# One core: row regions, written-out engine orders, late shared parts, routed rows added by VectorE

## The chip, the core and the metric

The kernel runs on one NeuronCore of a Trainium2 chip. The metric is the device time of one execution in microseconds. Three runs of the kernel before took 554.88, 562.25 and 564.08 us; the median is 562.25 us. What differs by less than 2% counts as no change.

## The reference, cut to what matters

8192 tokens (32 batches of 256) of 128 channels, all in float32:

```python
xn = layernorm(x)                       # without gain
# s: a recurrent block on xn
h = ln(xn)*g1+b1; hx = shift(h); xk, xv, xr = mixes of h and hx
k, v = xk @ Wk, xv @ Wv; sr = sigmoid(xr @ Wr)
scan over time: out_t = (e1*aa + e2*v)/(e1*bb + e2); aa, bb decay by exp(w), running max keeps it finite
x2 = xn + (sr*out) @ Wo
h2 = ln(x2)*g2+b2; xk, xr = mixes
s = x2 + sigmoid(xr @ Fr) * (relu(xk @ Fk)**2 @ Fv)       # 512 wide
# g: eight experts, each token goes to the one with the best logit
top = argmax(xn @ gate); score = sigmoid(max(xn @ gate))
g = silu( swiglu_shared(xn) + swiglu_expert[top](xn*score) )   # 256 wide
return x + s*g
```

## The kernel before, in words

The tokens are cut into 16 chunks of 512 (2 batches, 4 tiles of 128). All five engines run their own list of instructions and meet at semaphores.

**Front.** For each chunk SyncE loads x, VectorE takes the statistics (L921, L927), GpSimd makes 1/std with a power (L803 to L809), ScalarE normalises (`first_xn`, L580), TensorE transposes (L341), ScalarE copies the transpose to `XT` (L586), and TensorE makes the router's logits (L351). VectorE chooses each token's expert, and only when all 16 chunks are there it counts, per expert, how many tokens lie before each one, and so which row of the DRAM table `tokens_by_expert` each token gets (`routing_counts`, `routing_starts`, `routing_rows`, L960 to L988). The table has 71 tiles of 128 rows; it is first filled with padding rows by one DMA of 4686 KB.

**Steps.** Then come 18 steps, the same function `step(i)` on each engine. Step i advances the recurrent block of three chunks at once: z1 transpose, key, value, receptance of chunk i+1 (L366 to L387), the scan of chunk i on VectorE (L1010 to L1054), attention output, second norm, `ffn_key` of chunk i-1 (L396 to L419), `ffn_value` of chunk i-2 (L427). Each step has eight places where other work is filled in by `plan()`: in steps 0 to 5 the shared expert's 32 half parts (L449, L455 gate and up, L437 down, L1106), while GpSimd sends the rows to the table with one indirect DMA for each of 64 tiles (L849), 12 in a step; in steps 6 to 14 the 71 expert slots; in the last three steps the final sums.

**An expert slot** loads a tile of rows and its expert's weights (SyncE), scales the rows by the score (ScalarE, L683), transposes them (L478), multiplies by gate and up (L471), takes silu (L692) and the product (VectorE, L1114), multiplies by down (L485), copies out (L700), and scatters the rows to `routed_out` (GpSimd, L857).

**End.** For each chunk TensorE adds the routed rows and the shared output in PSUM by two products with the identity (L498, L499), ScalarE takes silu (L707), VectorE multiplies by s (L1121). Chunks 0 to 11 are added to a copy of x in DRAM by GpSimd's accumulating DMA (L868); the other four are added on VectorE and stored by SyncE. The block of the squares: `relu` of four quarters on ScalarE (L658), squares of quarters 0 and 2 on ScalarE (L666), of 1 and 3 on VectorE (L1090). The present token's weight comes from a tanh (L616), and needs the two 1024-wide products L1046 and L1049.

## Time and profile before

| | |
|---|---|
| three runs | 554.88, 562.25, 564.08 us |
| profiled execution | span 552.1 us from first to last instruction; its own device time isn't listed apart from these runs |
| PE | 477.2 us busy, 86% |
| VectorE | 401.3 us, 73% |
| ScalarE | 353.4 us, 64% |
| GpSimd | 279.0 us, 51% |
| granted TensorE clock, mean | 0.977 |
| DMA | 64.97 MB, 118 GB/s over the span |

A float32 matmul leaves two records in this trace (L471 has 568 for 284 products), a transpose one. Records overlap, since matmuls are pipelined: the time that one takes out of TensorE is the distance from its start to the next start, not its length.

### The profile page before, as it was taken

What the parts mean: (1) busy time and instruction counts of PE and PEld (TensorE: products, weight loads), DVE (VectorE), ACT (ScalarE), POOL (GpSimd) and SP (SyncE); (2) the same over time, 40 slices, a digit from 0 to 9 for tenths busy, and PEclk for the clock granted to TensorE, in tenths of its full rate; (3) what the DMA queues carried; (4) which work ended last, traced back from release to release, by engine and by line L of the source; (5) the groups of instructions that cost most, each with busy time, mean ns of one, the idle gap of its engine ahead of it and who ended that gap; (6) DMA issues with size and microseconds to landing.
All of it is one profiled execution on the core that took longest, in us unless ns stands there. A gap on an engine that the chain in (4) does not pass through costs nothing. (4 is left out here: it accounts for less than half of the span.)

```text
span 552.1 us, 9051 instructions
## 1 busy us (share of the span) xinstructions
PE 477.2 (86%) x2687; PEld 356.4 (65%) x2687; DVE 401.3 (73%) x808; ACT 353.4 (64%) x707; POOL 279.0 (51%) x329
## 2 busy tenths in 40 slices
PE   1989877879998789979898989898989898869796
PEld 1989444547575556569686868686868777644454
DVE  3553697858795877858696969797878788875345
ACT  4777424656663748576878686969696968554542
POOL 7565003565756375735273737363646464634440
PEclk9999898998999999989999999999999999999799
DMA  6339508210101010126363737373737372438395
GB/s 210 102 89 248 121 0 300 108 42 13 44 20 44 1 49 12 49 55 174 114 202 111 208 106 207 101 216 94 225 100 211 102 207 92 118 115 134 69 184 109
DMA packets 62592, 64.97 MB, mean 118 GB/s; under 512 B 5776, under 2 KB 50705, under 8 KB 62496
## 3 DMA queue, kind: packets, MB, share of 16 engines
q1 hardware_dynamic: 50736, 51.16, 32.5%
q0 software_dynamic: 10656, 11.68, 9.3%
q10 hardware_dynamic: 1152, 1.56, 0.9%
q8 instruction: 22, 0.36, 0.3%
q14 instruction: 26, 0.21, 0.1%
HBM read 46.86 MB, written 21.12 MB: 123 GB/s over the span
## 5 line engine op out<-in xcount | busy, mean ns | idle before, releaser
L857 POOL DMA_INDIRECT routed_out<-xh,xs x71 | 91.1, 1283 | 52.5 <-ACT xh L700 34.9
L849 POOL DMA_INDIRECT tokens_by_expert<-xn,pos x64 | 70.3, 1098 | 35.1 <-issue 18.5
L471 PE MATMUL bank_ring<-xh,ew 128*128 128x128 f32 x568 | 76.8, 279 | 0.0
L471 PEld LDWEIGHTS bank_ring<-xh,ew 128*128 128x128 f32 x568 | 70.8, 194 | 4.5 <-issue 3.8
L1090 DVE TENSOR_TENSOR kk<-rk 128x512 f32<-128x512 f32 x32 | 24.2, 755 | 61.2 <-ACT rk L658 55.6
L427 PE MATMUL bank_out<-fvw,kk 128*128 128x128 f32 x512 | 67.5, 278 | 0.0
L427 PEld LDWEIGHTS bank_out<-fvw,kk 128*128 128x128 f32 x512 | 63.4, 195 | 3.9 <-issue 3.9
L692 ACT ACTIVATE px<-bank_ring 128x256 f32<-128x256 f32 x71 | 27.1, 381 | 36.7 <-PE bank_ring L471 31.3
L831 POOL TENSOR_SCALAR x_sm<-x_mv 128x4 f32<-128x4 f32 x16 | 4.0, 247 | 81.4 <-DVE x_mv L1071 81.4
L485 PE MATMUL bank_ring<-ew,hx 128*128 128x128 f32 x284 | 43.5, 276 | 0.0
L387 PE MATMUL bank_fa<-xr,att 128*128 128x512 f32 x32 | 18.3, 656 | 24.6 <-ACT rk L658 23.8
L1114 DVE TENSOR_TENSOR hx<-px,bank_ring 128x256 f32<-128x256 f32 x71 | 29.1, 409 | 13.9 <-ACT px L692 13.9
L437 PEld LDWEIGHTS bank_ring<-sdn,hs 128*128 128x128 f32 x256 | 31.4, 194 | 11.9 <-issue 6.5
L455 PE MATMUL bank_ring<-xt,sup 128*128 128x512 f32 x64 | 34.8, 626 | 3.8 <-DVE hs L1106 3.8
L485 PEld LDWEIGHTS bank_ring<-ew,hx 128*128 128x128 f32 x284 | 37.3, 191 | 0.8 <-issue 0.7
L845 POOL TENSOR_TENSOR rw<-den_num,lq 128x512 f32<-128x512 f32 x16 | 20.2, 1262 | 33.8 <-issue 27.1
L449 PE MATMUL bank_ring<-xt,sup 128*128 128x512 f32 x64 | 34.3, 619 | 2.3 <-ACT tg L676 2.3
L419 PE MATMUL bank_fb<-xk,fkw 128*128 128x512 f32 x64 | 33.5, 604 | 1.8 <-issue 1.5
L437 PE MATMUL bank_ring<-sdn,hs 128*128 128x128 f32 x256 | 31.7, 278 | 3.4 <-DVE hs L1106 3.4
L700 ACT ACTIVATE xh<-bank_ring 128x256 f32<-128x256 f32 (+1 forms) x75 | 27.8, 371 | 9.6 <-PE bank_ring L485 6.8
L580 ACT ACTIVATE xn<-xi,nb,rs 128x128 f32<-128x128 f32 x64 | 26.3, 483 | 11.5 <-POOL nb L809 11.5
L419 PE MATMUL bank_fa<-xk,fkw 128*128 128x512 f32 x64 | 32.8, 594 | 0.0
(143 smaller groups left out, 1145.4 us busy)
## 6 DMA issues: line engine op xcount, KB each, us to landing
ew<-ex_w SPq DMA_DIRECT2D x71, 384.0 KB
xi<-x SPq DMA_DIRECT2D x20, 256.0 KB, 2.8
tokens_by_expert<-pad_row SPq DMA_DIRECT2D x1, 4686.0 KB, 20.4
xs<-tokens_by_expert SPq DMA_DIRECT2D x71, 66.0 KB
ew<-routed_out SPq DMA_DIRECT2D x16, 256.0 KB, 3.1
out<-xn POOLq DMA_DIRECT2D x12, 256.0 KB, 6.0
routed_out<-xh,xs POOLq DMA_INDIRECT x71, 2.9
tokens_by_expert<-xn,pos POOLq DMA_INDIRECT x64
```

The lines of the kernel that those rows point to most:

```text
L419: nc.tensor.matmul((FA, FB)[q % 2][:, :], part(FKW, q, P), XK2[:, :], start=True, stop=True)\
L427: last = nc.tensor.matmul(part(BO, j, CH), KK[:, q * CHUNK + j * P:q * CHUNK + (j + 1) * P], part(FVW, q, CH), start=(q + j == 0), stop=(q ...
L437: last = nc.tensor.matmul(part(b, j, CH), h[:, q * CHUNK + j * P:q * CHUNK + (j + 1) * P], part(SDN, q, CH), start=(q == 0), stop=(q == EQ ...
L449: nc.tensor.matmul(ring(5 * m + 3 * q)[:, :], part(SUP, q, P), part(XT, m, CHUNK), start=True, stop=True)\
L455: nc.tensor.matmul(ring(5 * m + 3 * q + 1)[:, :], part(SUP, EQ + q, P), part(XT, m, CHUNK), start=True, stop=True).then_inc(s_su, 1)
L471: last = nc.tensor.matmul(part(GU[n % 2], q, P), part(w, q, P), xt[:, 0:P], start=True, stop=True)
L485: last = nc.tensor.matmul(BX[:, P:P + CH], part(h, q, P), part(w, 2 * EQ + q, CH), start=(q == 0), stop=(q == EQ - 1))
L692: nc.scalar.activation(PX[n % 2][:, :], GU[n % 2][:, 0:EF], ACT.Silu).then_inc(s_px, 1)
L700: nc.scalar.activation(XH[n % NXH][:, a:b], BX[:, a:b], ACT.Copy).then_inc(s_xh, 1)
L849: nc.gpsimd.indirect_dma_start(xs_dram, bass.IndirectOffsetOnAxis(ap=POS[:, t:t + 1], axis=0), XN[:, t * XROW:(t + 1) * XROW], None).then_ ...
L857: nc.gpsimd.indirect_dma_start(routed_dram, bass.IndirectOffsetOnAxis(ap=XS[(n - 2) % NXS][:, CH:CH + 1].bitcast(i32), axis=0), XH[n % NXH ...
L1114: nc.vector.tensor_tensor(HX[n % NHX][:, :], PX[n % 2][:, :], GU[n % 2][:, EF:2 * EF], ALU.mult)\
```

## The change

It does many things at once.

- **Row regions.** Every expert has a region of 8320 rows of its own in the DRAM table, plus seven spare tiles. A row's place no longer depends on the counts of all experts, so rows are chosen after every four chunks (`expert_choice`, `expert_rows`), and their scatters can be sent from then on. Padding is 7 spare tiles and 8 tails of 66 KB in place of the 4686 KB fill. SyncE reads each tile's first row from a table.
- **Written-out orders.** `plan()`, `fill` and `step` go; each engine's calls are written out one by one. The first norm, the shared parts and the recurrent block's first chunks are interleaved. Between the first two and the last two of the 71 slots stand 15 slots to 2 chunks.
- **Late shared parts.** Shared parts of chunks 11 to 15 come after the last expert slot; their down products accumulate onto the routed rows in the same bank.
- **Routed rows on VectorE.** For chunks 0 to 10 VectorE adds routed rows to the shared output; for 11 to 15 one identity product stays.
- **Arithmetic moved.** Score scaling goes from ScalarE to GpSimd, all four squares to ScalarE, three small operations of the first norm from GpSimd to VectorE; exp with a clamp takes the place of tanh, and one 1024-wide VectorE operation goes. Receptance has two buffers and may run further ahead.
- 13 chunks, not 12, are added in DRAM; x is copied to the output before the routing is known.

```diff
+GROUPS = CHUNKS // GROUP
 
 XTILES = TILES + EXPERTS - 1
+REGION = TOKENS + P
+SPARE = XTILES - TILES
+XROWS = EXPERTS * REGION + SPARE * P
 XROW = CH + 4
...
+EARLY = 11
+ADDED = 13
+SUMS = list(range(CHUNKS))
+ON_VECTOR = (0, 1, 2, 3, 4, 5, 6, 7, 8, 9, 10)
...
+            sp.wait_ge(s_pad, 2)
+            sp.dma_start(xs_dram[EXPERTS * REGION:XROWS, :].rearrange("(n p) c -> p n c", p=P),
+                         PAD[:, :].unsqueeze(1).to_broadcast([P, SPARE, XROW])).then_inc(s_fill, 16)
...
-                if c == CHUNKS - 1:
-                    sp.wait_ge(s_pad, 2)
-                    sp.dma_start(xs_dram.rearrange("(n p) c -> p n c", p=P),
-                                 PAD[:, :].unsqueeze(1).to_broadcast([P, XTILES, XROW])).then_inc(s_fill, 16)
...
+                r = nc.sync.value_load(ROW[0:1, n:n + 1], min_val=0, max_val=XROWS - P)
+                sp.dma_start(XS[n % NXS][:, :], xs_dram[bass.ds(r, P), :]).then_inc(s_xs[n % NXS], 16)
...
-            sp.wait_ge(s_rt, RT_DONE)
+            sp.dma_start(out[0:ADDED * CHUNK // 2, :], x[0:ADDED * CHUNK // 2, :]).then_inc(s_pre, 16)
+            sp.dma_start(out[ADDED * CHUNK // 2:ADDED * CHUNK, :], x[ADDED * CHUNK // 2:ADDED * CHUNK, :]).then_inc(s_pre, 16)
+            sp.wait_ge(s_map, 1)
+            for e in range(EXPERTS):
+                r = nc.sync.value_load(PADS[0:1, e:e + 1], min_val=0, max_val=EXPERTS * REGION - P)
+                sp.dma_start(xs_dram[bass.ds(r, P), :], PAD[:, :]).then_inc(s_tail, 16)
...
             def receptance(c):
                 pe.wait_ge(s_mix, 3 * c + 3)
-                if c > 1:
-                    pe.wait_ge(s_rk, 4 * c - 5)
+                if c > 2:
+                    pe.wait_ge(s_rk, 4 * (c - 3) + 3)
...
+            def late_part(m, q):
+                if (m, q) == (EARLY, 0):
+                    pe.wait_ge(s_hx, XTILES)
+                    pe.wait_ge(s_xh, XTILES + 4)
+                else:
+                    pe.wait_ge(s_tg, 2 * m + q)
+                nc.tensor.matmul(RING[0][:, :], part(SUP, q, P), part(XT, m, CHUNK), start=True, stop=True)\
+                  .then_inc(s_sg, 1)
+                pe.wait_ge(s_hs, 2 * m + q)
+                nc.tensor.matmul(RING[1][:, :], part(SUP, EQ + q, P), part(XT, m, CHUNK),
+                                 start=True, stop=True).then_inc(s_su, 1)
...
-                    pe.wait_ge(s_hs, 2 * CHUNKS)
-                    pe.wait_ge(s_sh, CHUNKS)
+                    pe.wait_ge(s_hs, 2 * EARLY)
+                    pe.wait_ge(s_sh, EARLY)
...
-                    nc.tensor.matmul(b[:, :], ident, RR[c % 4], start=True, stop=False)
-                    nc.tensor.matmul(b[:, :], ident, part(XT, c, CHUNK), start=False, stop=True).then_inc(s_fy, 1)
...
+            def final_sum(m):
+                p = SUMS.index(m)
+                pe.wait_ge(s_fr_in[p % 4], 16 * (p // 4 + 1))
+                if any(n not in ON_VECTOR for n in SUMS[:p]):
+                    pe.wait_ge(s_fw, p)
+                else:
+                    pe.wait_ge(s_hx, XTILES)
+                    pe.wait_ge(s_xh, XTILES + 4)
+                b = RING[2]
+                nc.tensor.matmul(b[:, :], ident, RR[p % 4], start=True, stop=False)
+                if m < EARLY:
+                    nc.tensor.matmul(b[:, :], ident, part(XT, m, CHUNK), start=False, stop=True).then_inc(s_fy, 1)
+                    return
+                pe.wait_ge(s_hs, 2 * m + 2)
+                h = HS[m % 2]
+                for j in range(TPC):
+                    for q in range(EQ):
+                        last = nc.tensor.matmul(part(b, j, CH), h[:, q * CHUNK + j * P:q * CHUNK + (j + 1) * P],
+                                                part(SDN, q, CH), start=False, stop=(j + q == TPC + EQ - 2))
+                last.then_inc(s_fy, 1)
 
...
+            z1_transpose(5)
+            ffn_value(2, 0)
+            value(4)
+            ffn_value(2, 1)
+            expert_slot(3)
+            attention_out(3)
+            ffn_value(2, 2)
+            expert_slot(4)
+            ffn_value(2, 3)
+            expert_slot(5)
+            key(5)
+            receptance(5)
...
-            def tanh_d(c):
-                act.wait_ge(s_d, c + 1)
+                act.wait_ge(s_dc, c + 1)
                 if c > 0:
                     act.wait_ge(s_num, c)
-                nc.scalar.activation(TT, DD[:, :], ACT.Tanh, scale=0.5).then_inc(s_tt, 1)
+                nc.scalar.activation(QQ, DD[:, :], ACT.Exp).then_inc(s_q, 1)
 
...
-            def scale_rows(n):
-                act.wait_ge(s_xs[n % NXS], 16 * (n // NXS + 1))
-                xs = XS[n % NXS]
-                nc.scalar.activation(xs[:, 0:CH], xs[:, 0:CH], ACT.Identity, scale=xs[:, CH + 1:CH + 2])\
-                  .then_inc(s_xsc, 1)
...
+                if t % GT == 0:
+                    pool.wait_ge(s_pos, t // GT + 1)
+                    pool.wait_ge(s_sc, t // GT + 1)
...
+            def scale_rows(n):
+                pool.wait_ge(s_xs[n % NXS], 16 * (n // NXS + 1))
+                xs = XS[n % NXS]
+                nc.gpsimd.tensor_scalar(xs[:, 0:CH], xs[:, 0:CH], xs[:, CH + 1:CH + 2], None, ALU.mult).then_inc(s_xsc, 1)
...
+            def keep_logits(c):
+                dve.wait_ge(s_lg, c + 1)
+                nc.vector.tensor_copy(part(LG, c, TPC * E), BO[:, 0:TPC * E]).then_inc(s_lc, 1)
...
+            def expert_rows(g):
+                a, b = g * GT, (g + 1) * GT
+                first = CST[:, K_REG:K_REG + E] if g == 0 else part(BEGIN, g, E)
+                dve.wait_ge(s_th, g + 1)
+                nc.vector.tensor_scalar(rows_of_xn[:, a:b, CH + 1], part(SC, g, GT), 0.5, 0.5, ALU.mult, ALU.add)\
+                  .then_inc(s_sc, 1)
+                dve.wait_ge(s_rm, g + 1)
+                link(nc.vector.tensor_tensor(place, BO[:, 0:E], first, ALU.add))
+                link(nc.vector.tensor_tensor(part(BEGIN, g + 1, E), BO[:, E:2 * E], first, ALU.add))
+                link(nc.vector.tensor_tensor(cum, cum, place.unsqueeze(2).to_broadcast([P, E, GT]), ALU.add))
+                link(nc.vector.tensor_tensor(CUM, CUM, OH, ALU.mult))
+                link(nc.vector.tensor_reduce(POSF[:, a:b], CUM.rearrange("p (e j) -> p j e", e=E), AX.X, ALU.add))
+                nc.vector.tensor_copy(POS[:, a:b], POSF[:, a:b]).then_inc(s_pos, 1)
...
-                nc.vector.scalar_tensor_tensor(batches(DD[:, :]), before(PP), vec(V_FIRST), batches(BK[:, :]),
-                                               ALU.subtract, ALU.subtract).then_inc(s_d, 1)
-
-            def wkv_b(c):
+                    dve.wait_ge(s_q, c)
+                nc.vector.tensor_tensor(batches(DD[:, :]), batches(BK[:, :]), before(PP), ALU.subtract).then_inc(s_d, 1)
...
+            def present_value(c):
+                dve.wait_ge(s_q, c + 1)
+                dve.wait_ge(s_v, c + 1)
+                nc.vector.tensor_tensor(N2, QQ, BV[:, :], ALU.mult).then_inc(s_n2, 1)
...
-                tt = batches(TT).unsqueeze(1).to_broadcast([P, 2, BPC, SEQ])
-                nc.vector.scalar_tensor_tensor(dn, tt, 1.0, ba, ALU.add, ALU.mult).then_inc(s_w1b, 1)
-                dve.wait_ge(s_w1b, c + 1)
+                qv = QV[:, :].rearrange("p (k b t) -> p k b t", k=2, b=BPC)
                 dve.wait_ge(s_n2, c + 1)
-                nc.vector.tensor_tensor(DN[:, :], DN[:, :], TV[:, :], ALU.subtract).then_inc(s_num, 1)
+                nc.vector.tensor_tensor(dn, ba, qv, ALU.add).then_inc(s_num, 1)
...
-            def ffn_square(c, q):
-                dve.wait_ge(s_rk, 4 * c + q + 1)
-                if q == 1 and c > 0:
-                    dve.wait_ge(s_kv, c)
-                rk = part(RK, 1, CHUNK)
-                nc.vector.tensor_tensor(part(KK, q, CHUNK), rk, rk, ALU.mult).then_inc(s_kd, 1)
...
+            def final_sum(m):
+                p = SUMS.index(m)
+                dve.wait_ge(s_fr_in[p % 4], 16 * (p // 4 + 1))
+                dve.wait_ge(s_sh, m + 1)
+                nc.vector.tensor_tensor(part(XT, m, CHUNK), part(XT, m, CHUNK), RR[p % 4], ALU.add).then_inc(s_fd, 1)
```

## Rows read from the trace of the kernel before

**Rows 1.** Windows: PE, PEld, DVE, ACT, POOL busy (count), clock, DMA share, GB/s.

```profile
0.00:62.00 62.00, 47.19 (x206) 42.96 (x206) 30.21 (x159) 38.08 (x91) 33.98 (x87) 1.00 0.65 171
62.00:243.00 181.00, 155.19 (x723) 96.83 (x723) 140.14 (x240) 103.70 (x169) 95.42 (x99) 0.97 0.17 56
243.00:478.00 235.00, 214.33 (x1530) 181.62 (x1529) 191.33 (x341) 176.59 (x390) 122.75 (x120) 0.99 0.51 152
478.00:552.00 74.00, 60.52 (x232) 34.96 (x230) 39.58 (x70) 34.98 (x59) 26.84 (x24) 0.92 0.62 114
```

**Rows 2.** The chain that ended last: start us, us, what.

```profile
499.70 0.86 PE bank_ring L499 x2
502.27 0.89 PE bank_fb L408 x8
```

**Rows 3.** Timeline of TensorE, front and one expert slot: start us, us, instruction.

```profile
44.20 1.09 PE L341 MATMUL bank_out<-consts,xn 128*128 128x128 f32 x4
45.09 1.71 PE L351 MATMUL bank_fb<-gw,xt 128*128 128x8 f32 x8
46.65 1.09 PE L341 MATMUL bank_v<-consts,xn 128*128 128x128 f32 x4
...
250.33 1.06 PE L471 MATMUL bank_ring<-xh,ew 128*128 128x128 f32 x8
251.22 0.27 PE L478 MATMUL bank_ring<-consts,xs 128*128 128x128 f32 x1
251.33 0.61 PE L485 MATMUL bank_ring<-ew,hx 128*128 128x128 f32 x4
251.78 1.06 PE L427 MATMUL bank_out<-fvw,kk 128*128 128x128 f32 x8
```

**Rows 4.** Timeline of TensorE, one whole step of the expert stretch.

```profile
270.84 1.05 PE L396 MATMUL bank_fb<-att,rw 128*128 128x128 f32 x8
...
296.94 1.10 PE L387 MATMUL bank_fa<-xr,att 128*128 128x512 f32 x2 [1.81 <-ACT rk L658]
297.87 1.05 PE L396 MATMUL bank_fb<-att,rw 128*128 128x128 f32 x8
```

**Rows 5.** Groups by line and form: busy us, mean ns, idle before.

```profile
L683 ACT ACTIVATE xs<-xs 128x128 f32<-128x128 f32 x71 | 28.0, 398 | 0.0
...
L1090 DVE TENSOR_TENSOR kk<-rk 128x512 f32<-128x512 f32 x32 | 24.2, 755 | 61.2 <-ACT rk L658 55.6 <-issue 5.6
...
L1049 DVE TENSOR_TENSOR den_num<-den_num,tanh_d_and_value 128x1024 f32<-128x1024 f32 x16 | 19.6, 1225 | 0.6
```

**Rows 6.** The same view, GpSimd's scatters.

```profile
L857 POOL DMA_INDIRECT routed_out<-xh,xs x71 | 91.1, 1283 | 52.5 <-ACT xh L700 34.9 <-issue 17.6
...
L849 POOL DMA_INDIRECT tokens_by_expert<-xn,pos x64 | 70.3, 1098 | 35.1 <-issue 18.5 <-DVE kk L984 16.6
```

**Rows 7.** Timeline of GpSimd: the first scatter, then one step's small work.

```profile
83.74 1.27 POOL L849 DMA_INDIRECT tokens_by_expert<-xn,pos  x1 [16.56 <-DVE kk L984]
...
275.16 0.23 POOL L831 TENSOR_SCALAR x_sm<-x_mv 128x4 f32<-128x4 f32 x1 [5.20 <-DVE x_mv L1071]
...
277.01 1.04 POOL L823 TENSOR_TENSOR d<-h 128x512 f32<-128x512 f32 x1
278.21 1.81 POOL L857 DMA_INDIRECT routed_out<-xh,xs  x1 [0.17 <-issue]
...
295.73 1.26 POOL L845 TENSOR_TENSOR rw<-den_num,lq 128x512 f32<-128x512 f32 x1 [1.80 <-issue]
```

**Rows 8.** Timeline of VectorE: a scan that starts beside GpSimd's L823.

```profile
277.20 1.93 DVE L1034 TENSOR_TENSOR_SCAN bb_aa<-e,ev 128x514 f32<-128x514 f32 x1
```

**Rows 9.** By source: L823, then L1034: ns min/median/max, first and last start.

```profile
L823 POOL TENSOR_TENSOR d<-h x16: 1033/1040/2003, 51.1 to 466.2; 128x512 f32<-128x512 f32 x16
...
L1034 DVE TENSOR_TENSOR_SCAN bb_aa<-e,ev x16: 1202/1751/1956, 71.8 to 490.9; 128x514 f32<-128x514 f32 x16
```

**Rows 10.** Timeline of TensorE, its last matmul.

```profile
546.21 1.02 PE L499 MATMUL bank_ring<-xt,consts 128*128 128x512 f32 x2
```

More of the change, by code:

```diff
@@ L27 @@
 NEG = -1e38
+DMAX = 40.0
 NXS, NEW, NXH, NHX, AHEAD = 12, 5, 8, 3, 4
@@ new lines, in _ @@
+            pe.wait_ge(s_w, 16 * 3)
+            first_transpose(0)
+            z1_transpose(0)
+            logits(0)
+            first_transpose(1)
+            pe.wait_ge(s_wa, 16 * 5)
+            shared_part(0, 0)
+            logits(1)
+            first_transpose(2)
+            pe.wait_ge(s_wa, 16 * 5)
+            key(0)
+            logits(2)
+            first_transpose(3)
+            receptance(0)
+            value(0)
+            logits(3)
+            first_transpose(4)
+            z1_transpose(1)
@@ new lines, in _ @@
+            receptance(2)
+            shared_part(5, 0)
+            routing_prefix(2)
+            z1_transpose(3)
+            first_transpose(15)
+            logits(14)
+            value(2)
+            shared_part(5, 1)
+            pe.wait_ge(s_half, 1)
+            attention_out(0)
+            logits(15)
+            shared_part(6, 0)
+            routing_prefix(3)
+            shared_part(6, 1)
+            z2_transpose(0)
+            key(3)
+            shared_part(7, 0)
+            ffn_key(0, 0)
@@ new lines, in _ @@
+            ffn_key(4, 3)
+            ffn_value(4, 1)
+            expert_slot(18)
+            attention_out(5)
+            ffn_value(4, 2)
+            expert_slot(19)
+            ffn_value(4, 3)
+            expert_slot(20)
+            receptance(7)
+            key(7)
+            expert_slot(21)
+            z2_transpose(5)
+            value(7)
+            expert_slot(22)
+            z1_transpose(8)
+            ffn_receptance(5)
+            ffn_key(5, 0)
+            expert_slot(23)
@@ new lines, in _ @@
+            key(9)
+            expert_slot(36)
+            z2_transpose(7)
+            value(9)
+            expert_slot(37)
+            z1_transpose(10)
+            ffn_receptance(7)
+            ffn_key(7, 0)
+            expert_slot(38)
+            ffn_key(7, 1)
+            ffn_key(7, 2)
+            expert_slot(39)
+            ffn_key(7, 3)
+            ffn_value(7, 0)
+            expert_slot(40)
+            attention_out(8)
+            expert_slot(41)
+            receptance(10)
@@ new lines, in _ @@
+            ffn_key(8, 3)
+            ffn_value(8, 1)
+            expert_slot(48)
+            attention_out(9)
+            ffn_value(8, 2)
+            expert_slot(49)
+            ffn_value(8, 3)
+            expert_slot(50)
+            receptance(11)
+            key(11)
+            expert_slot(51)
+            z2_transpose(9)
+            value(11)
+            expert_slot(52)
+            z1_transpose(12)
+            ffn_receptance(9)
+            ffn_key(9, 0)
+            expert_slot(53)
```

2142 lines of the change are left out of this document (1692 added, 450 removed).

## The prediction, made before the result was known

> **What bounds the kernel now.** I read the windows first, cut where the work changes: the first norm (0 to 62), the stretch with shared parts and scatters (to 243), the 71 expert slots (to 478), the end (to 552) [rows 1]. TensorE is the busiest engine in all four, but its busy time overstates its load, so I price it by distances between starts. A 512-wide product takes 0.86 us, four 128-wide ones 0.89 [rows 2]. In the front, four transposes take 0.89 (44.20 to 45.09) and a chunk's logits 1.56 (45.09 to 46.65); an expert slot takes 1.45 (250.33 to 251.78), 0.11 of it for one transpose [rows 3].
>
> From these a chunk costs, beside its front: z1 and z2 transposes 0.44 each, key, value and receptance 2.58, attention output 0.89, FFN receptance 0.89, four keys 3.44, sixteen value products 3.56: together 12.2 us. Its shared part costs 5.2 (four at 0.86, eight at 0.22), its two identity products 1.7. The whole program: 16 x (2.45 + 12.2 + 5.2 + 1.7) = 345, and 71 x 1.45 = 103: 448 us of 552. So 104 us are idle or at the lower clock.
>
> Where they lie: one step in the expert stretch runs from 270.84 to 297.87, 27.0 us [rows 4], with 12.2 + 8 x 1.45 = 23.8 us of matmuls. 3.2 us are lost, 1.8 of them in one wait of the receptance for ScalarE's last relu, which stands behind a table load, Ln and Exp. Over the 8.7 steps from 243 to 478 that is some 28 us. The front to 243 holds 16 x 2.45 + 16 x 5.2 + six chunks x 12.2 = 195 us: 48 are lost, most of them before 97, where the first scatter waited 16.6 us for VectorE's routing and started only at 83.7 [rows 7]. The rest is lost at the end, whose clock is 0.92 [rows 1].
>
> **The change part by part.**
>
> *The identity products.* 32 become 5: 27 x 0.86 = 23 us less for TensorE, all in the end, where TensorE is what bounds. VectorE gets 11 sums of the form of L1090 (0.755 us, 0.6 by distance): 7 us, on an engine busy for 39.6 of the last 74 us [rows 1, 5]. TensorE's total becomes 448 - 23 = 425 us.
>
> *Arithmetic.* VectorE loses two squares (1.5 us) and one 1024-wide operation (1.2) per chunk [rows 5]. The clamp is new: no row has it; between half and all of L1090's 0.755, I take 0.45, as it is one pass over the same 512 columns. Net -2.2 us per chunk. ScalarE loses 0.40 per slot for the scaling [rows 5] and gains two squares, near 0.6 each by L1090's size: 7.5 x 0.4 - 1.2 = 1.8 us less per chunk. Exp for tanh I cost at nothing (ScalarE has 58 of 235 us free). Both are off the path; they shorten what stands ahead of the waits in the step.
>
> *GpSimd's scaling.* No row has 128 x 128 there. Nearest are L831 (4 columns, 0.23) and L823 (512 columns, two inputs, 1.04) [rows 7]: between 0.23 and 1.04; on the line between them 0.43, which I take. A scatter out takes (91.1 + 17.6)/71 = 1.53 with its issue time [rows 6]. Per chunk: 7.5 x (1.53 + 0.43) = 14.7, and the norm's small operations with d1, 275.16 to 278.21, 3.1, and rw 1.3 [rows 7]: 19.1 us, below the 23 of TensorE. With 1.04 per row it would be 23.7.
>
> *The front.* Rows of chunks 0 to 3 can be sent once logits 0 to 3 and one small routing round are done. VectorE has 30.2 us up to 62 now, for 16 norms, four choices and chunk 0 up to its differences [rows 1]; its new list has 11 norms with five more small operations each, one choice, chunk 0 to its scans and three half parts ahead of the first rows, which I put at 36; the x loads and the hops between engines make it about 45 (ends: 40, and 84 as now). From there GpSimd's one queue sets the pace: 64 scatters at (70.3 + 18.5)/64 = 1.39 make 89 [rows 6]; among them stand five powers (5.5), three rw (3.8), and three rounds of the small operations and d1 (9.3): 108 us, to 153. Then landing, SyncE's loads of rows, and the first scaling, which the run shows only in pieces: 7 us. The slots start at **160**, against 243. Does the rest fit under it? TensorE has 16 x 2.45 + 11 x 5.2 + 32 for parts of chunks 0 to 4 = 128; VectorE 170.3 now to 243 [rows 1], less ten late products (7), less 2.5 chunks x 18.7 ((191.3 - 29)/8.7) = 47, less 8 for lighter arithmetic, plus some 10 for more small routing and norm operations: 119. Both fit. The smaller fill (4686 KB to 7 tiles and 8 tails) and the earlier copy of x leave the queue before loads that matter; eight tails and 71 row lookups on SyncE are covered, since a slot leaves it over 3 us and needs two issues.
>
> *The slots.* Between first and last stand 15 slots to two chunks: 12.2 + 7.5 x 1.45 = 23.1 us of matmuls per chunk. The relus no longer stand behind Ln and Exp and the receptance waits for an older relu, so its 1.8 us goes; what comes next is ScalarE's silu and copy, which TensorE needs within the slot. I keep 1.4 us of loss: 24.5 (ends: 23.1 and 27.0). From slot 0 to slot 72 TensorE's list has 71 x 1.45 + 119.5 of chunk work = 222 us; at 23.1/24.5 it takes **241**, to 401.
>
> *The end.* After slot 72 stand 44 us of chunk work, ten half parts at 1.72 (17) and five final sums at 0.86 + 1.78 (13): 74 us. VectorE has 65 in the same stretch: 11 sums, 19 final operations and ten half parts at 0.6 are 24, and 2.5 chunks at 18.7 - 2.2 are 41. The last chunks' recurrences have nothing left to hide behind but these. I take 85, the share of idle time of the present end with less clock lost (ends: 79 and 95). From TensorE's last matmul (547.2) to the end of the span are 4.9 us now [rows 10]; I take 5.
>
> **Sum:** 160 + 241 + 85 + 5 = 491 us of span, against 552.1. The fastest run is 2.8 above that span and the median 10.1; I add 6: **497 us**.
>
> **A rule against it.** An L823 of 1.04 us at 277.01 and a scan beside it from 277.20, which took 1.93 where its least is 1.20; L823 itself goes from 1.03 to 2.00 [rows 7, 8, 9]. So the two engines hold each other up, for about the length of one instruction, and the change gives GpSimd 71 more instructions on SBUF. The Trainium skill, SBUF — State Buffer, section SBUF: two separate sides, has it that a VectorE operation with two SBUF inputs, or in a two-port mode, and a GpSimd operation that reads SBUF exclude each other for the whole instruction; by that rule the trace agrees, and a clamp in a two-port mode would also hold back GpSimd's descriptors.
>
> **The rivals.**
> - *The ports bite.* Ten GpSimd operations per chunk (7.5 scalings and three others) each wait 0.7 us, the delay of that scan: 19.1 + 7 = 26.1 us per chunk, 241 x 26.1/24.5 = 257: 513. Against: 108 of 235 us are free on GpSimd, and not every one meets a long operation. 0.05.
> - *Late front.* Four engines in fixed order hold VectorE's first routing round to 80, as now [rows 7]: slots start at 195, 532. For: VectorE was idle half of the first 62 us [rows 1]. Against: 36 us of work. 0.12.
> - *The step stays at 27.0* per chunk because another wait replaces the receptance's: 241 x 27.0/24.5 = 266: 522. 0.13.
> - *All goes well:* start 150, 231 for the slots, 79 at the end: 150 + 231 + 79 + 5 + 6 = 471. 0.08.
> - *Nothing gained.* Late front, step of 27.0, and an end of 95: 195 + 266 + 95 + 5 + 6 = 567, within 2%. 0.04.
> - *Slower.* GpSimd becomes the bound of the slots: every operation of it, scatters included, is doubled, as the longest L823 was: 38 us per chunk, 241 x 38/24.5 = 374: 630. It decides from 32 us per chunk on (1.7 times), where 573 is passed. Against: the mean scatter was 1.28 and 1.10, with VectorE at 81% [rows 1, 6]. 0.03.
> - The forecast: 0.55.
>
> **Range and chances.** About 2% can be told from no change. The range takes in the forecast, both neighbours at 513 and 522, the good case at 471 and the late front at 532: 470 to 533. Faster: all cases but "nothing gained" and "slower", 0.93; same 0.04; slower 0.03.
>
> **What would show it.** In the changed profile: the first scatter near 45 us and the last near 153; the first L1114-like product near 160; starts of attention outputs 24.5 us apart on average between slots 7 and 67; last expert product near 401; GpSimd's scaling near 0.43 us; TensorE's last matmul near 486. The prediction is wrong if the slots start after 195, if the chunks are 27 us apart, or if GpSimd is over 90% busy between 160 and 401.

## The result, and the profile after

The changed kernel took 527.49 us (median of four runs, 519.34 to 530.05), the kernel before 558.57 us on the same chip (four runs, 552.61 to 564.08). The ratio is 0.947, 95% interval 0.933 to 0.960: faster. The ratio goes by the runs within 1.5% of the fastest of their kernel (519.34 and 526.38 of the changed one), and the profiled run, 528.60, isn't one of them. The forecast was 497 from a median of 562.25, a gain of 65 us; 31 were measured. The profiled execution has a span of 526.8 us against 491 forecast; 35.8 us have to be found.

The page of the changed kernel (busy time, then tenths in 40 slices):

```profile
PE 448.2 (85%) x2645; PEld 336.9 (64%) x2645; DVE 398.6 (76%) x907; ACT 339.1 (64%) x661; POOL 329.9 (63%) x347
...
PE   0968969788199989899999989998999887497995
...
DVE  4599978488348289968996896799599989884452
...
PEclk9979968859779999999999999999999998798998
```

GpSimd has 51 us more than before, as scaling came to it. TensorE has two thin places, slice 11 (132 to 145) and slice 35 (448 to 461), and the clock is low around both and around 100 to 120. By windows, cut where the work changes as [rows 1] are (columns as there):

```profile
0.00:62.00 62.00, 41.98 (x199) 28.68 (x200) 48.37 (x230) 35.63 (x79) 36.97 (x38) 0.94 0.34 104
62.00:185.00 123.00, 98.45 (x456) 66.12 (x455) 78.53 (x192) 61.94 (x113) 82.45 (x84) 0.82 0.27 87
185.00:418.00 233.00, 221.26 (x1558) 184.16 (x1557) 199.74 (x357) 178.56 (x362) 174.49 (x189) 1.00 0.52 153
418.00:526.00 108.00, 86.47 (x437) 57.90 (x436) 72.00 (x131) 62.94 (x110) 35.95 (x38) 0.92 0.44 79
```

The start moved from 243 to 185 and the stretch of slots kept its length (233 against 235), although 71 scalings moved and the mixture of work in it is other. The end grew from 74 to 108, as it now holds the late shared parts that stood in the front. The same by source (ns least, median, most; first and last start): expert products, scatters, scalings, first powers, scans of the weighted values, sums on VectorE, clamps, and the product that makes z1.

```profile
L480 PE MATMUL bank_ring<-xh,ew x568: 272/275/275, 185.3 to 418.5; 128*128 128x128 f32 x190
...
L1607 POOL DMA_INDIRECT tokens_by_expert<-xn,pos x64: 957/962/1932, 50.1 to 174.4; - x64
...
L1614 POOL TENSOR_SCALAR xs<-xs x71: 598/713/1882, 180.6 to 406.6; 128x128 f32<-128x128 f32 x71
...
L1572 POOL TENSOR_TENSOR rs<-ve,minus_half x16: 1627/1642/2483, 8.3 to 74.8; 128x8 f32<-128x8 f32 x16
...
L2081 DVE TENSOR_TENSOR_SCAN bb_aa<-e,ev x16: 1214/1216/1229, 45.4 to 470.6; 128x514 f32<-128x514 f32 x16
...
L2172 DVE TENSOR_TENSOR xt<-xt,ew x11: 656/684/1761, 432.5 to 465.7; 128x512 f32<-128x512 f32 x11
...
L2066 DVE TENSOR_SCALAR dd<-dd,vectors x16: 485/486/829, 29.9 to 465.3; 128x512 f32<-128x512 f32 x16
...
L2036 DVE TENSOR_TENSOR z<-xn,r x16: 668/1255/2136, 13.2 to 410.4; 128x512 f32<-128x512 f32 x16
```

The scalings by group (busy us, mean ns, idle before):

```profile
L1614 POOL TENSOR_SCALAR xs<-xs 128x128 f32<-128x128 f32 x71 | 58.3, 825 | 6.3 <-DMA xs<-tokens_by_expert 4.6
```

So against the forecast's terms: start 185.3 for 160 (+25), slots 233 for 241 (-8), end from 418.5 to 526.8, 108 for 90 (+18).

What the thin place at 132 to 145 is, the timelines of TensorE, ScalarE and VectorE say (start us, us, instruction; in brackets the idle time before it and who ended it):

```profile
133.22 1.12 PE L414 MATMUL bank_fb<-xk,fkw 128*128 128x512 f32 x2 [1.73 <-issue]
134.19 1.02 PE L414 MATMUL bank_fa<-xk,fkw 128*128 128x512 f32 x2
145.25 2.08 PE L414 MATMUL bank_fb<-xk,fkw 128*128 128x512 f32 x2 [10.05 <-ACT rk L999]
...
144.60 0.60 ACT L999 ACTIVATE rk<-bank_fb 128x512 f32<-128x512 f32 x1 [11.44 <-remote]
...
150.85 0.69 DVE L2146 TENSOR_TENSOR hs<-tg,bank_ring 128x512 f32<-128x512 f32 x1 [14.49 <-PE bank_ring L464]
```

TensorE issued the key product at 133.2, and ScalarE, whose relu needs nothing else that was still open, started only at 144.6. "remote" stands where the profile names no instruction that ended at that time. I call this a late count: TensorE's count of a finished product (its semaphore) reached the others late. That the product itself ended late can't be excluded, as the ends of matmuls are modelled. TensorE then waited for ScalarE's relu and VectorE for the shared part behind: one such stop, and three engines stand for 10 to 14 us. All such rows of the list of waits, 60 to 200:

```profile
ACT rk L999 <- remote: 12.2, 2, 11.4
ACT xt L930 <- remote: 6.3, 1, 6.3
DVE rt L1999 <- remote: 4.8, 1, 4.8
DVE ew L1972 <- remote: 4.1, 2, 3.0
ACT tf L993 <- remote: 2.4, 1, 2.4
```

The thin place in the end, TensorE and VectorE:

```profile
445.59 1.02 PE L444 MATMUL bank_ring<-xt,sup 128*128 128x512 f32 x2
454.53 2.07 PE L447 MATMUL bank_ring<-xt,sup 128*128 128x512 f32 x2 [7.91 <-DVE hs L2157]
...
450.88 0.66 DVE L2172 TENSOR_TENSOR xt<-xt,ew 128x512 f32<-128x512 f32 x1
451.46 1.22 DVE L2097 TENSOR_TENSOR den_num<-bb_aa,q_and_q_value 128x1024 f32<-128x1024 f32 x1
452.60 0.68 DVE L2178 TENSOR_TENSOR xn<-xt,xn 128x512 f32<-128x512 f32 x1
453.20 0.68 DVE L2102 SCALAR_TENSOR_TENSOR den_num<-tr,den_num 128x512 f32<-128x512 f32 x1
453.80 0.68 DVE L2157 TENSOR_TENSOR hs<-tg,bank_ring 128x512 f32<-128x512 f32 x1
```

TensorE waits 7.9 us for the late product of chunk 11, which stands on VectorE behind final sums (L2172), final products (L2178) and a recurrence. This was the first suspect for the end, and the very thing that the title of the change puts there.

### The profile page after: what moved, and what is told of

It reads as the page before. It is cut to its first block, busy times and chain, and to the rows that moved or that the text cites. A ratio compares the mean times of both kernels' runs of the same rounds, so it can differ in the third digit from the quotient of the medians.

```text
span 526.8 us, 9495 instructions
## 1 busy us (share of the span) xinstructions
PE 448.2 (85%) x2645; PEld 336.9 (64%) x2645; DVE 398.6 (76%) x907; ACT 339.1 (64%) x661; POOL 329.9 (63%) x347
## 4 chain that ended last, share of the span: by engine, by line
PE 38%; ACT 9%; DVE 4%; issue 4%; POOL 1%; ACTq 0%; POOLq 0%; DVEq 0%
PE bank_ring L480 8%; PE bank_out L424 6%; PE bank_ring L494 4%; PE bank_fb L414 4%; PE bank_fa L414 3%; PE bank_fb L391 2%; PE bank_k L367 2%; PE bank_fb L403 1%; PE bank_fb L397 1%; PE bank_ring L487 1%; PE bank_fa L382 1%; PE bank_ring L447 1%; PE bank_ring L444 1%; PE bank_ring L515 1%; ACT e L953 1%
## 5 line engine op out<-in xcount | busy, mean ns | idle before, releaser
L1619 POOL DMA_INDIRECT routed_out<-xh,xs x71 | 81.4, 1147 | 43.9 <-issue 24.6
L1607 POOL DMA_INDIRECT tokens_by_expert<-xn,pos x64 | 67.9, 1061 | 21.1 <-issue 21.1
L480 PE MATMUL bank_ring<-xh,ew 128*128 128x128 f32 x568 | 74.9, 275 | 0.0
L1614 POOL TENSOR_SCALAR xs<-xs 128x128 f32<-128x128 f32 x71 | 58.3, 825 | 6.3 <-DMA xs<-tokens_by_expert 4.6
L1005 ACT ACTIVATE kk<-rk 128x512 f32<-128x512 f32 x64 | 40.3, 650 | 0.7
L1572 POOL TENSOR_TENSOR rs<-ve,minus_half 128x8 f32<-128x8 f32 x16 | 28.5, 1786 | 15.7 <-DVE ve L1936 15.6
L978 ACT ACTIVATE z<-x,x_sm 128x128 f32<-128x128 f32 x64 | 26.4, 482 | 17.0 <-POOL x_sm L1592 16.9
L464 PE MATMUL bank_ring<-xt,sup 128*128 128x512 f32 x44 | 28.9, 745 | 3.3 <-DVE hs L2146 3.3
L2146 DVE TENSOR_TENSOR hs<-tg,bank_ring 128x512 f32<-128x512 f32 x22 | 15.0, 680 | 20.4 <-PE bank_ring L464 16.5
L1631 POOL DMA_DIRECT2D out<-xn x13 | 17.2, 1831 | 19.1 <-DVE xn L2178 18.0
```

Source lines behind the costliest of these rows:

```text
L464: nc.tensor.matmul(ring(5 * m + 3 * q + 1)[:, :], part(SUP, EQ + q, P), part(XT, m, CHUNK), start=True, stop=True).then_inc(s_su, 1)
L480: last = nc.tensor.matmul(part(GU[n % 2], q, P), part(w, q, P), xt[:, 0:P], start=True, stop=True)
L1005: nc.scalar.activation(part(KK, q, CHUNK), part(RK, q % 2, CHUNK), ACT.Square).then_inc(s_kk, 1)
L1572: nc.gpsimd.tensor_tensor(RS[:, a:b], VE[:, a:b], NH[:, 0:2 * TPC], ALU.pow).then_inc(s_rs, 1)
L1607: nc.gpsimd.indirect_dma_start(xs_dram, bass.IndirectOffsetOnAxis(ap=POS[:, t:t + 1], axis=0), XN[:, t * XROW:(t + 1) * XROW], None).then_ ...
L1614: nc.gpsimd.tensor_scalar(xs[:, 0:CH], xs[:, 0:CH], xs[:, CH + 1:CH + 2], None, ALU.mult).then_inc(s_xsc, 1)
```

## The experiments

Seventeen runs (e1 and e13 are the changed kernel itself), in groups that share one chip and their runs of the kernel before. Ratios are to that kernel, with their 95% intervals.

**First group: is it there again, and what do the sums cost.** The kernel before took 547.46.

> The changed kernel once more, as a control. In its profile TensorE stood still from 134.6 to 144.6 (fourth key of chunk 0 waits for a relu whose product had been issued at 134.2) and had a late count at 96 to 106. If the program sets these two stops (its instructions, its order), they come again within 3 us of the same places and the slots start at 185 +- 3. If they are accidents of one execution (a page of DRAM, a refresh), they are gone or elsewhere, the slots start near 170, and that profile is some 10 to 15 us shorter. Ratio to the kernel before 0.947 +- 0.013.

No edit. 509.46 us, ratio 0.929 (0.925 to 0.934), span 508.0. Its expert products, and its one wait of TensorE over 4 us in the front:

```profile
L480 PE MATMUL bank_ring<-xh,ew x568: 272/275/275, 169.3 to 401.2; 128*128 128x128 f32 x190
...
142.65 1.11 PE L397 MATMUL bank_fb<-consts,z 128*128 128x128 f32 x4 [5.20 <-ACT z L978]
```

Not one row of "remote" stands between 60 and 200. The start is 16 us earlier, slots (231.9) and end (106.8) are as they were. So 16 of the 35.8 us belong to the execution, not to the program. Against its own kernel before (547.46) the changed one gains 38 us here, still far from 65.

> The named part of the change alone is undone: the sums of chunks 0 to 10 are two identity products each on TensorE (11 x 2 x 0.86 = 19 us more for it), and VectorE has eleven operations of 0.6 less. My prediction: TensorE bounds the end, so the end is 19 us longer: 546, ratio to the kernel before 0.98. Rival A: VectorE bounds 432 to 454 (the 7.9 us wait of TensorE for the late product), so the products fill TensorE's idle time there: only 19 - 12 = 7 us longer, 534. Rival B: the sums on VectorE cost more than they spare: 527 or less.

```diff
-ON_VECTOR = (0, 1, 2, 3, 4, 5, 6, 7, 8, 9, 10)
+ON_VECTOR = ()
...
@@ tensor @@
 ffn_receptance(12)
+final_sum(0)
 ffn_key(12, 0)
+final_sum(1)
...
```

521.46 us, ratio 0.952 (0.948 to 0.957): 12.0 us more than e1, for 19 us of products. Slots 167.7 to 399.6; all of it lies in the end. Between my sum (19) and rival A (7): TensorE bounds the end for most of the time, not all of it. Its waits after the last slot add up to 11.8 us here and to 17.3 in e1, so 5.5 us of the products went into waits. The named part of the change is worth 12 us.

> 24 products of 8 columns (four instructions each, 96 in all, into a bank that nothing reads) stand ahead of TensorE's list, where it waits for the first x anyway. Theory, code loading: the stops at 96 and 134 stand where TensorE's next block of 256 instructions is fetched, so that both move 96 instructions earlier in its list (the second one from the third key of chunk 0 to before the first shared part of chunk 6, near 118), or vanish. Rival, the queue of transfers: the stop at 134 stands beside the eight tail writes of SyncE (133 to 148) and stays with them. Rival, the order: it stays at the fourth key of chunk 0. Time: 527 +- 8 by each, as one stop takes the place of the other; 517 if they vanish.

```diff
 pe.wait_ge(s_w, 16 * 3)
+for _ in range(24):
+    nc.tensor.matmul(RING[2][:, 0:EXPERTS], ident, GW[:, :], start=True, stop=True)
```

513.60 us (0.936), start 173.3, 4 us behind e1. No late count at all, here as in its control: inconclusive.

> SyncE writes the eight tails of 66 KB after the first five blocks of expert weights (384 KB each) instead of before them. Theory, the queue of transfers: with 8 x 128 short rows no longer at 133 the stop of TensorE at 134.6 to 144.6 goes, slots start near 175, 517 us. Rival, code loading or order: the stop stays within 3 us, 527 +- 8, and only the weights land earlier (before 149).

```diff
-for e in range(EXPERTS): ...  # eight tails
 for n in range(NEW):
     load_weights(n)
+for e in range(EXPERTS): ...
```

510.74 us (0.932), start 169.6: the place of the tails is worth nothing. On the late counts it is as inconclusive as e3.

**Second group: the end.** Before 546.55.

> VectorE's late product (11, 0) stands ahead of the first final sum instead of behind ten sums, nine final products and den_num. In the control (508.0) TensorE waits for it in the end and runs at the lower clock after. Theory, the named wait is the cause: TensorE goes on about 8 us earlier, 501. Rival, VectorE's load is the cause (it is busy without a gap for 22 us there, with z2 of chunk 13 and the mixes of chunk 15 behind the same work): the wait only moves to the next step, 508 +- 2. From the times of both: what TensorE needs next, z2 of chunk 13, came 1.7 us after the late product, so I expect the rival, ratio to the kernel before 0.929 +- 0.004.

```diff
@@ vector @@
 channel_mixes(12)
+late_part(11, 0)
 final_sum(0)
...
-late_part(11, 0)
 time_mixes(15)
```

510.85 us (0.934; 0.932 to 0.937). This group has no control of its own; e8, whose end is untouched, took 509.37. As the rival had it: the named wait is gone and the next one stands in its place, as long.

```profile
436.55 1.11 PE L397 MATMUL bank_fb<-consts,z 128*128 128x128 f32 x4 [8.84 <-ACT z L978]
```

> Part left out: VectorE's eleven final sums add one column instead of 512, so chunks 0 to 10 of the output lack nearly all of the routed part; waits and order are unchanged. If VectorE bounds 413 to 437, this is 11 x 0.45 = 5 us shorter, of which 8 or 9 sums stand in the stretch: 504. If the sums lie beside other work, as my prediction had it (7 us on VectorE, hidden), no change: 508.

```diff
-nc.vector.tensor_tensor(part(XT, m, CHUNK), part(XT, m, CHUNK), RR[p % 4], ALU.add)
+nc.vector.tensor_tensor(XT[:, m*CHUNK:m*CHUNK+1], XT[:, m*CHUNK:m*CHUNK+1], RR[p % 4][:, 0:1], ALU.add)
```

510.72 us (0.936; 0.933 to 0.938): nothing gained. Even without the width of the sums TensorE waits 7.71 us at 435.8. On VectorE:

```profile
425.72 0.69 DVE L2179 TENSOR_TENSOR xn<-xt,xn 128x512 f32<-128x512 f32 x1 [0.93 <-ACT xt L1041]
...
427.52 0.68 DVE L2135 SCALAR_TENSOR_TENSOR xi<-tf,bank_out 128x512 f32<-128x512 f32 x1
...
430.58 0.67 DVE L2112 TENSOR_TENSOR x<-bank_fb,xn 128x512 f32<-128x512 f32 x1
```

The freed time became idle time (0.93 here): in 413 to 435 VectorE is busy for 16.85 us, against 21.75 in e1, and 3.5 us of the rest it waits for ScalarE's silu of the final sums (L1041). And x2 of chunk 13 (L2112) still came at 430.6, 5 us after its product, behind s of chunk 12 (L2135) and a scan. My theory that the sums themselves make the end long fell, and with it the simpler one that VectorE's load does: with 4.9 us less of it TensorE still waits. What holds x2 back here is its place in VectorE's list, which e9 changes.

> The same sums and final products by the same engines, but those of chunks 5 to 10 come after the last recurrence, where VectorE idles (20 of the last 67 us in the control), with chunks 11 and 12 between them; the late product (11, 0) first and d1 of chunk 15 ahead of the norm of chunk 13. If VectorE's load in 413 to 437 is the cause of the long end, 12 operations of 0.6 leave it: 7 us and what the lower clock took there (1 to 3): 499. If the end is bound by the chain of recurrences through ScalarE's table loads, nothing: 508. If the stores or ScalarE's order become late: slower, up to 513.

```diff
-SUMS = list(range(CHUNKS))
+SUMS = [0, 1, 2, 3, 4, 11, 5, 6, 12, 7, 8, 9, 10, 13, 14, 15]
@@ vector @@
 make_tn(15)
+final_sum(5)
+final_sum(6)
+final_sum(7)
+final_sum(8)
...
```

The late product (11, 0) and d1 of chunk 15 move forward as well.

514.12 us (0.940; 0.937 to 0.943), 3 to 5 us slower than its neighbours. The reason named last fits: moved that far, the sums hold up the final sums of TensorE, which run in one order with them and now wait 3.3 us for ScalarE's L1041. TensorE's waits after the last slot add up to 20.5 us, against 17.1 in e5, and its clock there is 0.90.

```profile
436.14 1.11 PE L397 MATMUL bank_fb<-consts,z 128*128 128x128 f32 x4 [8.52 <-ACT z L978]
...
474.56 2.05 PE L507 MATMUL bank_ring<-ew,consts 128*128 128x512 f32 x2 [3.30 <-ACT xt L1041]
```

> Front, GpSimd's order: rw of chunk 2 and the norm's small operations of chunk 1 stand four scatters earlier. In the control their inputs are there at 132.2 and they start at 138.4, and TensorE waits 5.2 us for z2. If TensorE sets the start of the slots, it comes 5 us earlier (164); if the scatters and loads behind them set it (last scatter 157.4, first scaled rows 165), 0 to 2.5 us: start 167 to 169. I expect the latter: 507, not to be told from no change; TensorE's wait for z2 of chunk 1 below 1 us.

```diff
@@ gpsimd @@
 scatter_rows(47)
+make_rw(2)
+rstd_of_x2(1)
...
 scatter_rows(51)
-make_rw(2)
-rstd_of_x2(1)
```

509.37 us (0.933), start 168.3 for 169.3: no change that can be told, as expected. TensorE's wait for z2 of chunk 1 is gone (no wait over 0.2 us between 130 and 150) and the start did not follow: scatters and loads set it.

**Third group: two edits of the order, and the scaling.** Before 553.74. Late counts in all four: "remote" rows add up to 29 to 35 us in 60 to 200, the slots start at 179.8 to 182.3. So these are compared by stage: last slot to the end of the span.

> End. Leaving the sums out (e6), moving them later (e7) and the late product forward (e5) shortened nothing: in all of them z2 of chunk 13 came at 436 to 438, as x2 of chunk 13 stands on VectorE behind s of chunk 12 and a scan, 3 to 7 us after its product (425), and GpSimd's norm and d1 of chunk 15 behind that. Here x2 of chunk 13 stands ahead of them, the late product (11, 0) ahead of the sums, d1 of chunk 15 and the norm of chunk 13 ahead of the stores of chunks 5 to 7, and z2 of chunk 13 ahead of ScalarE's eighth final part. Theory, the chain of chunk 13 sets TensorE's wait of 8.3 us: it shrinks to about 3, 503 (ratio to the kernel before 0.920). Rival, the chain of chunk 15 (its recurrence, weighted values to tn) sets the end: 508 to 510 as it is now (0.930).

```diff
@@ vector @@
 channel_mixes(12)
+late_part(11, 0)
 final_sum(0)
...
 final_sum(7)
+make_x2(13)
...
@@ gpsimd @@
 final_store(4)
+make_d1(15)
+rstd_of_x2(13)
...
```

ScalarE's and VectorE's final parts of chunk 8 move back behind z2 of chunk 13 and the mixes.

523.51 us (0.947; 0.943 to 0.951); end 413.3 to 520.6, 107.3 against 106.8 in e1. The wait for z2 is 5.2, where it was 8.8 in e5, another joined it, and nothing was gained. VectorE had no gap in the stretch: 21.75 of 22 us busy (the window below, columns as above). TensorE's timeline, then the window:

```profile
446.36 1.12 PE L397 MATMUL bank_fb<-consts,z 128*128 128x128 f32 x4 [5.20 <-ACT z L978]
448.86 2.07 PE L367 MATMUL bank_k<-xk,att 128*128 128x512 f32 x2 [1.39 <-DVE xk L2044]
```

```profile
425.00:447.00 22.00, 12.79 (x67) 8.47 (x68) 21.75 (x38) 16.81 (x30) 12.55 (x13) 0.94 0.97 195
```

> End. ScalarE's fourth relu of chunk 13 stands ahead of the table load, Ln, Exp and second table load for chunk 15 (4 us) instead of behind them. In the control TensorE waits 3.1 us for that relu before the attention output of chunk 14, then works without a wait to the last product but for 0.7 us. Theory, every wait of TensorE there is paid in full: 505 (0.924). Rival, the late product (13, 0), which ScalarE's four microseconds now stand ahead of, makes TensorE wait instead: 508 (0.930).

```diff
@@ scalar @@
-preload("natural_log_exp_and_others"); inverse_of_den(15); preload("silu_and_others")
 ffn_relu(13, 3)
 late_part(12, 1)
 ffn_square(13, 3)
 final_part(11)
+preload("natural_log_exp_and_others"); inverse_of_den(15); preload("silu_and_others")
```

521.47 us (0.943; 0.938 to 0.948), end 415.6 to 520.6: 105.0. TensorE's wait of 3.1 us is gone, waits of 0.9 and 0.3 came; 2 us gained of 3. (Nine profiles of kernels whose end was not changed have ends of 106.7 to 110.1 us.)

> The reordering of e8 (rw of chunk 2 and norm of chunk 1 four scatters earlier), of e9 and of e10 together. If the waits of the end are paid by themselves, 508 - 5 - 3 - 1 = 499 (0.913); if one of them takes the place of the other, 503 (0.920).

Edit: e8, e9 and e10 together. 519.16 us (0.936; 0.929 to 0.942), end 103.0: 3.8 us less than in e1, more than e9 and e10 gave one by one.

> One part undone: the 71 scalings of rows are done by ScalarE (0.40 each in the kernel before) instead of GpSimd (0.83 on average in the changed one), each right behind the copy of its slot. My prediction: ScalarE has room and so has GpSimd, so that the place of the scaling is off the path: slots from 169 to 401 as before, 508 (0.930). Rival, ScalarE's silu and copy, which TensorE needs within the slot, come 0.4 us later in each: 1 us per chunk more, 518 (0.947). Rival, the ports: with 71 fewer operations of GpSimd on SBUF VectorE's longest operations (2.0 us against 0.7 to 1.2) get rarer, and the slots take 3 us less: 505.

```diff
@@ scalar @@
+def scale_rows(n):
+    act.wait_ge(s_xs[n % NXS], 16 * (n // NXS + 1))
+    nc.scalar.activation(xs[:, 0:CH], xs[:, 0:CH], ACT.Identity, scale=xs[:, CH + 1:CH + 2])...
@@ gpsimd @@
-scale_rows(n)   # all 71
```

526.03 us (0.952; 0.948 to 0.956). Slots 180.3 to 416.9, 236.6 us, against 233.5 and 233.8 in e9 and e10: the scaling on GpSimd is worth 3 us, a third of the 10 that the first rival had. The rival of the ports has the wrong sign on balance. VectorE is busy for 202.0 us in the slots without the scalings and for 198.2 (e9) and 199.1 (e10) with them, so no cost of theirs shows on VectorE either.

**Fourth group.** Before 546.88.

> The changed kernel again, as the control of this group. The chips so far are of two kinds: on two of them the kernel before takes 547 us and the changed one, where it ran, 509 (0.929), with no late count of TensorE; on two others the kernel before takes 554 to 559 and changed kernels 519 to 527, with late counts in the front (4 to 10 us before 150) and slots that start 12 to 16 us later. If the late counts belong to the chip, this is either 509 and start 169, or 522 and start 180; the ratio 0.929 or 0.943.

510.75 us, 0.933 (0.931 to 0.935), start 168.5, no "remote" row.

> As all three reorderings together (e11), and the sums and final products of chunks 6 to 8 stand behind the mixes of chunk 15 and of chunk 13. In e9 VectorE was without a gap from 425 to 452 and TensorE's key of chunk 15 waited for the mixes (1.4) behind z2 (5.2). If VectorE's load bounds that stretch, 6 operations of 0.6 less ahead of the mixes give 3 to 4 us beyond e11; if the chain of chunk 15 behind them bounds, nothing. I expect 2 us less than e11.

```diff
@@ vector, on top of e11 @@
...
 channel_mixes(13)
+final_sum(6)
+final_sum(7)
+final_sum(8)
 final_sum(9)
 running_max(15)
+final_part(6)
+final_part(7)
 differences(15)
+final_part(8)
 final_part(9)
...
```

The same calls go from their old places, and ScalarE's final parts 6 and 7 move back behind z2 of chunk 13.

504.14 us, ratio 0.923 (0.919 to 0.926): the fastest of all, 6.6 us below its control. Key of chunk 15 follows z2 without a wait:

```profile
433.39 1.11 PE L397 MATMUL bank_fb<-consts,z 128*128 128x128 f32 x4 [5.26 <-ACT z L978]
434.30 1.91 PE L367 MATMUL bank_k<-xk,att 128*128 128x512 f32 x2
```

> The 24 small products ahead of TensorE's list (96 instructions) once more. On a chip with late counts they stood, in three kernels with the same TensorE list, before 91, 107 and 149. Code loading: the places in the list move 96 instructions earlier or the counts are in time; anything else: the same products are late again. On a chip without them it tells nothing new: 4 us above the control.

512.15 us (0.936), again without late counts: inconclusive a second time.

> The three reorderings together, beside their control now. In its first run the end from the last slot took 103.0 us against 106.8, 107.3 and 106.7 of the control, e9 and e12. 4 us below the control by that: ratio to it 0.992.

506.26 us, ratio 0.925 (0.923 to 0.928), 4.5 below its control: 0.991, as expected. From e16 to e14 are 2.1 us more, but the runs of both overlap (505.19 to 507.79, 503.39 to 506.84) and the ends in their profiles are 102.8 and 102.3: that moving the three sums helps further isn't shown.

**Fifth group.** Before 554.32.

> Part left out: GpSimd's first power takes the 4 columns of 1/sqrt(var + eps) and not the other 4 (the factor for z1 is 1 instead), so z1 of the attention part is scaled wrongly; waits and order are unchanged. In the control the power of 8 columns takes 1.64 (16 of them, 26 us), where my forecast had 1.1. Theory, this size is what makes the front late: 16 x 0.6 less on the engine that sets the first and the last scatter, of which 11 stand ahead of the first (where it waits for VectorE now and then) and 5 among the scatters: first scatter at 48 to 49 instead of 51.2, last 3 us plus that earlier, near 152, slots from 164 instead of 169. Rival, TensorE's list of shared parts sets the start: slots from 168 or 169, 509.

```diff
-nc.gpsimd.tensor_tensor(RS[:, a:b], VE[:, a:b], NH[:, 0:2 * TPC], ALU.pow)
+nc.gpsimd.tensor_tensor(RS[:, a:a + TPC], VE[:, a:a + TPC], NH[:, 0:TPC], ALU.pow)
```

518.90 us (0.937; 0.927 to 0.948, the widest interval of all). This chip is the one of the fourth group, where the kernel before took 546.9; now it takes 554.3 and counts come late. So the late counts do not belong to a chip, as I had thought in e13. The powers fell to 1.01 us, but the first scatter stayed at 50.9 and GpSimd waited for VectorE instead (25.0 us against 16.4):

```profile
L1573 POOL TENSOR_TENSOR rs<-ve,minus_half x16: 1006/1012/1852, 8.4 to 75.9; 128x4 f32<-128x4 f32 x16
...
  DVE ve L1937: 25.0, 11
```

The three longest late counts of this run, of eight rows in its list of waits:

```profile
ACT xt L930 <- remote: 5.9, 1, 5.9
DVE ew L1973 <- remote: 4.8, 2, 3.0
DVE hs L2147 <- remote: 4.8, 1, 4.8
```

The last scatter was at 167.9 and the start at 179.1, against 168.3 and 179.8 in e9. By this comparison (both with late counts, on two chips) the size of the power is not what makes the front late.

## Why the prediction was off, point by point

**The shape held.** The start moved forward, the slots kept their pace, TensorE stayed the engine that bounds, GpSimd took the scaling. Slots: 241 forecast, 232 to 234 measured in every run of this order. 241 was a slip: 222 at 23.1/24.5 is 236. The pace itself was right: from 183.4 to 379.6 the attention outputs of e1 start 24.5 us apart, as forecast. The other 4 us are work that I had placed in the slots and that stands behind them: at my prices the products recorded between first and last slot come to 217 us, not 222. "The ports bite" and "slower" did not come: GpSimd is busy for 174.5 of 233 us in the slots. Scaling has a median of 0.71 and a mean of 0.83, where I took 0.43, and was still hidden, as e12 shows. The scan of [rows 8, 9], with a median of 1.75 before, has 1.22 in the changed kernel, but the stall did not go: the product that makes z1 (L2036), never over 0.69 before (L995), now has a median of 1.26 and takes up to 2.14. Another instruction meets GpSimd's now, and the slots kept their pace all the same. Clamps at 0.49 (0.45) and sums at 0.68 (0.6 by distance) were as taken.

**Step "The front", 160.** In the profile shown it was 185.3. Sixteen of these 25 us go with late counts of TensorE, an effect that no row of before showed; that the counts, and nothing else in those sessions, cost the 16 us is likely and not shown. Over 18 profiles of kernels with the changed front it is either wholly there or wholly absent: "remote" rows between 60 and 200 add up to 0 in 12, and to 28 to 35 us in 6. The other 9 us are there without late counts too (169.3 and 168.5 in the two controls). By my terms: the first scatter at 51.2, not 45, although VectorE had just the work that I gave it (36.9 us busy to 51): it waited for others for 14 us, where I allowed 9. The 64 scatters with what stands among them, 106 us (51.2 to 157.4), where I had 108. From the last scatter to the first expert product 12 us (157.4 to 169.3), where I had 7. The rival "late front" had the right direction with another mechanism: it put the first scatter at 80.

**Step "The end", 85 and 5 to close.** This is the step of the forecast that failed by the program's own doing: "I take 85, the share of idle time of the present end". In e1 it took 101.0 (401.2 to 502.2) and 5.8. At my prices the products recorded there come to 78 us, not 74: the 4 us that the slots have less. TensorE's waits add up to 17.3 us, 8.3 of them in one place. By estimate the other 6 us went with the clock: it was 0.76 in 421 to 441, behind waits of 1 to 8 us. From 461 on TensorE worked without a wait but one of 0.7 us. So the 11 us that I allowed for idle time and clock were 23, and the share that I named did not give 11: the end of the kernel before holds 55 us of products in 69 (478 to 547.2), at which rate 74 make 93 and 78 make 98. I had also compared sums, 74 us of TensorE against 65 of VectorE, and let them overlap. But VectorE's 71 us of the end are not spread (e1, columns as above; in the third row it idles for 15 of 40 us):

```profile
413.00:435.00 22.00, 11.25 (x62) 7.41 (x62) 21.75 (x38) 15.29 (x26) 14.00 (x12) 0.92 0.97 196
421.00:441.00 20.00, 11.37 (x55) 7.41 (x54) 18.62 (x35) 10.27 (x20) 16.04 (x14) 0.76 1.22 196
441.00:481.00 40.00, 36.38 (x174) 23.30 (x173) 24.67 (x42) 27.67 (x45) 9.90 (x10) 0.99 0.41 60
```

In the full stretch the recurrences of chunks 14 and 15, x2 of chunk 13 and the finals stand in one queue, and TensorE's next three steps hang on three of them. Taking one away gives its time to the next: e5, e6 and e9 gained nothing, e10 2 us, e11, with e9 and e10 in one kernel, 3.8 us. Beside their control e16 and e14 show it best: TensorE's waits in the end fell from 17.3 us (e1) to 12.3 (e16) and 11.7 (e14), and the time by 4.5 and 6.6 us against the control's. So of some 17 us of waits the order of the lists is shown to cost about 5; for the rest it is argued from the timelines. One end is also not one number: e13, the same kernel, took 110.1 where e1 took 106.8. Behind the same wait of 3.1 us at 460 its clock was 0.80 for 15 us, against 1.00, and 2.5 of the 3.3 us lie between there and the next wait (34.3 us against 31.8).

**The identity products.** 23 us less for TensorE, all paid, was too much: e2 shows 12.0 us for 19, and 5.5 of the other 7 filled waits. For all 27 products at that rate 14 or 15 us would remain of the 23; that was not run. The 7 us on VectorE cost nothing by themselves (e6).

**The last 6 us.** I added 6 for the way from the span to the median. In the changed kernel the median was 0.7 above the profiled span and a run is 2 us longer than its span (528.6 for 526.8), so this made the miss smaller than the terms were.

**What stays open.** What makes TensorE's counts late, or its products, if it is they. It was seen in three of six groups of runs, on at least two chips, once present and once absent on the same chip; when it is there, the kernel before is slower too (553.7 to 558.6 against 546.6 to 547.5), and the ratio of the unedited changed kernel is 0.947, against 0.929 and 0.933. Its places are alike in three kernels of one group (near 90, 107 and 147 to 150), and in the two profiles of the other groups (near 100 and 106). The one profile of the kernel before comes from such a group and has no "remote" row in 60 to 200 (two in all, 1.9 and 1.6 us), so that what slowed it there is not seen either. Code loading and the tails were proposed; e3, e4 and e15 fell into groups without the effect and could not tell. Open also is which of the chains holds the last 5 us of z2's wait in e14.

## What to carry to other kernels

Two engines with 74 and 65 us of work in the last stretch do not give a stretch of 85: lay the busier parts side by side in time, and where the second engine is full for 20 us while the first waits, price that window by itself, by the order of its list as much as by its load. If you price a stretch by the idle share of an older one, work the share out. A wait that the profile names is only the first of several that end within a microsecond or two; before moving what it names, look up when the next instruction's inputs came. Profile a changed kernel a second time before explaining its stalls: nearly half of this miss (16 of 36 us) did not come again.

## What the runs showed of the hardware

- The engine that waits for a product of TensorE can start as late as 11 us after the product was issued, in the longest case with no instruction of TensorE recorded for 10 us: such waits stand in all six profiles of three sessions and in none of the twelve of the other three (0 us or 28 to 35 us in sum, nothing between). Only the word "remote" tells it from a wait of the program in a single profile.
- GpSimd's power takes 1.64 us for 128 x 8 and 1.01 for 128 x 4 (e17): it grows with its elements, and at 128 x 4 is five times the 0.20 us of the product beside it (L1592 of e1).
- GpSimd's product of 128 x 128 with a column takes 0.60 at least, 0.71 in the median and 1.88 at most beside a busy VectorE, more than half of the 1.04 of its 512-column subtraction [rows 7]. The Trainium skill, SBUF — State Buffer, section SBUF: two separate sides, lets one of the two engines wait for the other's whole instruction. The trace agrees: the three longest scalings (1.88, 1.83 and 1.74 us, at 391.0, 243.1 and 292.1) each began while VectorE's L2036, which has two inputs in SBUF, was running.
